# Three of sixteen drives per scan unit made by ScalarE on turned tiles, and the skip term and rectifier written to PSUM by ScalarE

## The reference

```
xp, z = split(x @ W_in)
xc    = silu(xprev * conv_w[0] + xp * conv_w[1] + conv_b)
dt_r, Bc, Cc = split(xc @ W_x)          # 8, 16, 16 columns
dt    = softplus(dt_r @ W_dt + b_dt)
for each state s:   h[t] = exp(dt[t] * A[s]) * h[t-1] + (dt[t] * xc[t]) * Bc[t, s]
                    y[t] += h[t] * Cc[t, s]
y     = (y + D * xc) * silu(z)
out   = y @ W_out
```

## Time and profile before

| what | value |
|---|---|
| median of 3 runs | 949.73 us |
| span of the profiled execution, first to last instruction | 947.3 us |
| PE busy | 834.3 us (88%) |
| DVE busy | 710.7 us (75%) |
| ACT busy | 508.3 us (54%) |
| POOL busy | 549.2 us (58%) |
| share of 16 DMA engines, the one data queue | 57.9% |

### The profile page before, as it was taken

How to read it: one execution, slowest core, us unless ns; L and a number is a source line. 1 busy time by engine, 2 the same in 40 slices (tenths; PEclk the granted TensorE clock), 3 DMA queues, 4 the chain that set the end, 5 groups by cost and what they waited for, 6 DMA issues and landing times. The chain is left out here.

```text
span 947.3 us, 10224 instructions
## 1 busy us (share of the span) xinstructions
PE 834.3 (88%) x3004; PEld 492.0 (52%) x3004; DVE 710.7 (75%) x767; ACT 508.3 (54%) x702; POOL 549.2 (58%) x373
## 2 busy tenths in 40 slices
PE   5579897979899898986687999989999999999996
PEld 1224342433334333332243555558888888888885
DVE  1999999999999999999965455546565665565664
ACT  4645666556566666643315446456555554555553
POOL 4678989999998998875736955312212211212210
PEclk9799999999999999997987999999999999999999
DMA  7969898889879898796609800002343342343341
GB/s 167 342 201 344 312 332 273 337 311 305 324 257 369 308 327 309 279 328 222 202 0 137 157 0 1 1 1 63 117 133 100 122 133 90 90 133 100 122 118 59
DMA packets 75349, 178.24 MB, mean 188 GB/s; under 512 B 24514, under 2 KB 25044, under 8 KB 75300
## 3 DMA queue, kind: packets, MB, share of 16 engines
q1 hardware_dynamic: 75316, 177.85, 57.9%
HBM read 175.57 MB, written 2.26 MB: 188 GB/s over the span
## 5 line engine op out<-in xcount | busy, mean ns | idle before, releaser
L455 POOL TENSOR_TENSOR prod<-hidden,c_wide 128x1024 f32<-128x1024 f32 x128 | 300.0, 2356 | 64.6 <-DVE hidden L888 60.5
L551 PE MATMUL ps_y<-prod,ident 128*128 128x512 f32 x512 | 244.2, 622 | 27.9 <-POOL prod L455 27.7
L888 DVE TENSOR_TENSOR_SCAN hidden<-decay,ps_d 128x1024 f32<-128x1024 f32 x92 | 209.9, 2281 | 8.3
L1920 PE MATMUL ps_conv<-hankel,u_high 128*128 128x512 f32 (+1 forms) x768 | 215.3, 361 | 0.0
L551 PEld LDWEIGHTS ps_y<-prod,ident 128*128 128x128 f32 x512 | 99.0, 198 | 169.2 <-issue 116.7
L1920 PEld LDWEIGHTS ps_conv<-hankel,u_high 128*128 128x128 f32 x768 | 138.6, 189 | 25.4 <-DVE u_t L1786 0.2
L1920 PE MATMUL ps_conv<-hankel,u_low 128*128 128x512 f32 (+1 forms) x384 | 138.1, 360 | 0.0
L2034 DVE TENSOR_TENSOR stack<-ps_conv,stack 64x512 fp32r<-64x512 f32 x128 | 88.2, 689 | 62.7 <-ACT stack L2001 60.2
L1751 POOL CAST block_mix<-even 128x256 fp32r (+1 forms) x32 | 12.7, 396 | 209.3 <-PE sums L1792 209.3
L2034 DVE TENSOR_TENSOR qk<-ps_conv,qk 64x512 fp32r<-64x512 f32 x128 | 88.2, 689 | 50.2 <-ACT qk L2001 47.5
L874 DVE TENSOR_TENSOR ps_d<-ps_x,b_wide 128x1024 f32<-128x1024 f32 x92 | 113.3, 1232 | 4.9 <-DMA b_wide<-bc_rows 0.4
(11 more groups left out here) (283 smaller groups left out, 1158.8 us busy)
## 6 DMA issues: line engine op xcount, KB each, us to landing
b_wide<-bc_rows SPq DMA_DIRECT2D x128, 512.0 KB, 5.6
c_wide<-bc_rows SPq DMA_DIRECT2D x128, 512.0 KB, 5.2
hankel<-filters SPq DMA_DIRECT2D x32, 1026.0 KB, 5.2
plus<-in_M_phi_plus SPq DMA_DIRECT2D x2, 1024.0 KB, 13.5
minus<-in_M_phi_minus SPq DMA_DIRECT2D x2, 1024.0 KB, 18.9
x_pair<-in_x SPq DMA_DIRECT2D x2, 768.0 KB, 8.5
bc_rows<-mixed_and_low SPq DMA_DIRECT2D x8, 128.0 KB, 5.4
out<-plus SPq DMA_DIRECT2D x4, 256.0 KB, 4.9
```

Of the source, the lines that this page charges most:

```text
L455: nc.gpsimd.tensor_tensor(prod[k % PAIR][:, :], hidden[k % DEEP][:, :], c_wide[s % BC_DEEP][:, :], ALU.mult).then_inc(prod_ready, 1)
L551: mm = nc.tensor.matmul(out, ident[:, :], halves(prod[k % PAIR])[h], start=False, stop=(k % N == N - 1))
L888: nc.vector.tensor_tensor_scan(hidden[k % DEEP][:, order], left[:, order], right[:, order], 0.0, ALU.mult, ALU.add).then_inc(hidden_ready, 1)
L1920: mm = nc.tensor.matmul(out, pairs[q][wp][:, 2 * delta + source, :], rows, start=(delta == 0 and term == 0), stop=(delta == 2 * half + 1 a ...
```

## The change

The drives of the states 4, 7 and 10 (`TURNED_STATES`) are no longer made by VectorE. `dtx` is turned once for each unit (tokens on partitions, 8 tiles of 128 by 128) together with B's rows; ScalarE copies both to SBUF (`dtx_t`, `b_t`). For each of the three states ScalarE then scales 8 tiles by one column of `b_t` each (a value for each token, `scale_drive`), and TensorE turns the 8 results back into `ps_d` (`turn_drive`), where the scan reads them. B's rows of these states are no longer spread by transfers, and the use of the `b_wide` buffers follows a table. The rectifier is written by ScalarE in place in `ps_w`, and `D * xc` is written by ScalarE into `ps_y`; TensorE adds onto both. `xc` is one buffer where there were two. In the last unit the shared states are 2 and 6 (before: 6) and the turned one is 7.

```diff
+TURNED_STATES = (4, 7, 10)
-        LAST_SHARE = POOL_STATES[2:3]
+        LAST_SHARE = (2, 6)
+        LAST_TURNED = (7,)
@@ TensorE
                 def gate_in(u, i, b):
-                    pe.wait_ge(dtx_ready, u)
+                    pe.wait_ge(dtx_t_ready, 3 * u)
                     project(i, b, w_gate[i], z_ready)
-                def add_rectified(u):
-                    pe.wait_ge(abs_ready, u + 1)
-                    pe.wait_ge(relu_ready, u)
-                    add_part(ident, rectified, start=True)
-                def skip_in(u, i):
-                    at_least(pe, gated_ready, u)
-                    for h, out in enumerate(halves(ps_y)):
-                        nc.tensor.matmul(out, skip[i][:, :], halves(xc[i])[h], start=True, stop=False)
+                def turn_dtx(u):
+                    def turn(half):
+                        for t in range(half * SPANS, (half + 1) * SPANS):
+                            mm = nc.tensor.transpose(ps_w[:, t * 128:(t + 1) * 128], dtx[:, t * 128:(t + 1) * 128], ident[:, :])
+                        mm.then_inc(dtx_turned, 1)
+                    pe.wait_ge(dtx_kept, u + 1)
+                    turn(1)
+                    for t in range(TILES):
+                        mm = nc.tensor.transpose(ps_w[:, t * C:(t + 1) * C], dt_low[BC_ROW:, t * 128:(t + 1) * 128],
+                                                 ident[BC_ROW:, BC_ROW:])
+                    mm.then_inc(dtx_turned, 1)
+                    pe.wait_ge(dtx_t_ready, 3 * u + 2)
+                    turn(0)
+                def turn_drive(u, s, last=False):
+                    scanned(u, s - 2)
+                    for half in range(2):
+                        pe.wait_ge(drive_t_ready, 2 * turned_before(u, s, last) + half + 1)
+                        for t in range(half * SPANS, (half + 1) * SPANS):
+                            mm = nc.tensor.transpose(ps_d[:, t * 128:(t + 1) * 128], drive_t[:, t, :], ident[:, :])
+                    mm.then_inc(drive_turned, 1)
...
                             if s == Y_LAG:
                                 if i == 0 and not first:
                                     out_product(b - 1)
+                                if Y_LAG + 1 in turned(not ahead):
+                                    turn_drive(u, Y_LAG + 1, not ahead)
+                                if i == 0 and not first:
                                     conv_in(v, j, bv)
-                                    pe.wait_ge(g.mixed_ready, b)
-                                skip_in(u, i)
...
-                                sum_states(n - Y_LAG, (k - Y_LAG) % (2 * N))
+                                sum_states(n - Y_LAG, (k - Y_LAG) % (2 * N), u if s == Y_LAG else None)
+                            if s > Y_LAG and s + 1 in turned(not ahead):
+                                turn_drive(u, s + 1, not ahead)
...
-                                if s == (7 if i == 1 or first else 5):
+                                if s == (7 if i == 1 or first else 6):
                                     scanned(u, WIDE_SHARED[1])
                                     low_rank(v, j)
...
-                                if s == 11:
-                                    add_rectified(v)
                                 if s == 12:
                                     add_exponential(v)
+                                if s == N - 1:
+                                    turn_dtx(v)
@@ ScalarE
+                def skip_in(u, i, taken=0):
+                    at_least(act, gated_ready, u)
+                    at_least(act, g.mixed_ready, taken)
+                    nc.scalar.activation(ps_y[:, :], xc[:, :], ACT.Copy, scale=cols[i][:, 1:2]).then_inc(skip_ready, 1)
...
-                        nc.scalar.activation(rectified[:, :], ps_w[:, :], ACT.Relu).then_inc(relu_ready, 1)
+                        nc.scalar.activation(ps_w[:, :], ps_w[:, :], ACT.Relu).then_inc(relu_ready, 1)
...
+                def take_turned(u):
+                    def take(n, half):
+                        act.wait_ge(dtx_turned, 3 * u + n + 1)
+                        nc.scalar.activation(dtx_t[:, half * SPANS:(half + 1) * SPANS, :].rearrange("p t d -> p (t d)"),
+                                             ps_w[:, half * H:(half + 1) * H], ACT.Copy).then_inc(dtx_t_ready, 1)
+                    at_least(act, drive_turned, TURNED * u)
+                    take(0, 1)
+                    act.wait_ge(dtx_turned, 3 * u + 2)
+                    nc.scalar.activation(b_t[:, :, :], ps_w[:, 0:H].rearrange("p (t c) -> p t c", c=C)[:, :, 0:N],
+                                         ACT.Copy).then_inc(dtx_t_ready, 1)
+                    take(2, 0)
+                def scale_drive(u, s, last=False):
+                    act.wait_ge(dtx_t_ready, 3 * u + 3)
+                    at_least(act, drive_turned, turned_before(u, s, last))
+                    for t in range(TILES):
+                        part = nc.scalar.activation(drive_t[:, t, :], dtx_t[:, t, :], ACT.Copy, scale=b_t[:, t, s:s + 1])
+                        if t % SPANS == SPANS - 1:
+                            part.then_inc(drive_t_ready, 1)
...
                                     else:
                                         norm_silu(nc, act, g, b - 1)
+                                skip_in(u, i, taken=b if i == 0 else 0)
                                 silu_input(v, j)
...
                                 decay_of(v, j, 1, last and i == 0)
+                                take_turned(v)
+                                if TURNED_STATES[0] in turned(last and i == 0):
+                                    scale_drive(v, TURNED_STATES[0], last and i == 0)
@@ VectorE
-                            if s in shared(final) and s in WIDE_SHARED:
-                                drive_step(u, s + 1, final)
-                            elif s not in shared(final) and not (s - 1 in shared(final) and s - 1 in WIDE_SHARED):
-                                drive_step(u, s, final)
+                            if s not in shared(final) + turned(final):
+                                drive_step(b, i, s, last)
```

More of the change, by code:

```diff
@@ L249, in mamba_stage @@
         soft = sb("soft", [D, L])
[L250 removed]
+        dtx_t = sb("dtx_t", [128, TILES, D])
+        drive_t = sb("drive_t", [128, TILES, D])
+        b_t = sb("b_t", [128, TILES, N])
         minus_ident = sb("minus_ident", [128, 128])
[L252 removed]
         one_plus = a.late[:, 0:L]
@@ L307, in shared_before, with turned_before, spread_order, b_slot @@
             return SHARE * u + sum(p < s for p in shared(last))
+        def turned_before(u, s, last=False):
+            return TURNED * u + sum(p < s for p in turned(last))
+        def spread_order(last):
+            return [(i, s) for i in range(2) for s in range(N) if s not in turned(last and i == 1)]
+        SLOT_ORDER = (0, 1, 2, 3) * 2 + (0, 1, 2) + (0, 1, 2, 3) * 3 + (0, 1, 2)
+        def b_slot(i, s, last):
+            at = spread_order(last).index((i, s))
+            return SLOT_ORDER[at] if at < len(SLOT_ORDER) else at - len(SLOT_ORDER)
+        def b_loads(b, i, s, last):
+            slot = b_slot(i, s, last)
+            rank = sum(b_slot(j, p, last) == slot for j, p in spread_order(last) if (j, p) < (i, s))
+            return 16 * (b * SLOT_ORDER.count(slot) + rank + 1)
         def own_states(last):
@@ L383, in unit @@
                     for s in range(N):
-                        spread_b(u, i, s)
+                        if s not in turned(u == 2 * B - 1):
+                            spread_b(u, i, s)
                         if u or s:
@@ L752, in batch @@
                                 decay_of(u, i, t, final)
+                            if t in turned(final) and t != TURNED_STATES[0]:
+                                scale_drive(u, t, final)
                             if t == N and not final:
@@ L962, in _ @@
                 nc.vector.tensor_scalar(minus_ident[:, :], ident[:, :], -1.0, None, ALU.mult).then_inc(minus_ready, 1)
-                for i in range(2):
-                    nc.vector.tensor_scalar(skip[i][:, :], ident[:, :], cols[i][:, 1:2], None, ALU.mult).then_inc(diag_ready, 1)
                 first_dt()
```

99 lines of the change are left out of this document (59 added, 40 removed).

## The result

The changed kernel takes 980.69 us (median; 978.97 to 982.32) where the kernel before takes 950.81 us (949.38 to 952.35) on the same chip: ratio 1.0311, 95% interval 1.0279 to 1.0343. The forecast was 977.5 us in a range of 956 to 1003.

What follows compares the result with a forecast made beforehand. VectorE was taken to bound the stage at 54.0 us a unit, GpSimd close behind. Forward units +0.6, backward +15.0, clock +14.1 and ends -1.7 made +28.0 on 949.7: 977.5 us, range 956 to 1003.

Steps and rivals of the forecast that it cites:

- Term 1: Boundary between units: sums and gate's projection stand behind the turning, scan 2 comes late; +1.8 us per unit with a successor.
- Term 2: Scan 7 in a forward unit waits for its turned drive: +2.3 us; such a unit +0.2 us in all.
- Term 3: Backward unit: input projection queued behind a sum awaiting the skip term; scans 6, 7, 10 late by 3.7, 2.1, 1.8 us.
- Term 4: TensorE's clock falls behind idle times: +1.7 us in three backward units, +1.5 us at six boundaries.
- The ends: Opening unit +0.7 us, last unit -2.4 us for two drives less and no gate's projection.
- (a): Turned drives come in time, so the kernel gets faster: some -25 us, 925 us; chance 0.10.
- (b): Transposes are no activity for TensorE's clock, which falls at each boundary: 998 us; chance 0.20.
- (c): TensorE's clock stays high everywhere while the late scans stand: 963 us; chance 0.17.
- (d): Weight loads don't hide behind transposes, 0.2 us more on each: +25 us more, over 1000; chance 0.04.
- (e): Late scans are made up since GpSimd and TensorE have caught up: near no change, 950 us; chance 0.06.

Runs made afterwards that it cites:

- Run 1: Changed kernel with TensorE turning `dtx` and B's rows behind the sum of state 13 instead of ahead of it: 963.01 us.
- run 2: Changed kernel with the input projection ahead of the first sum in backward units too, unit 1 left as it was: 969.29 us.
- run 6: Kernel before with only the skip product replaced by ScalarE's write of the skip term to `ps_y`, no turned drives: 961.90 us.
- run 10: Kernel before with the skip term written by ScalarE, and the input projection ahead of the first sum in all units but the opening one: 950.68 us.
- run 3: Changed kernel with two useless pairs of 512-column products on TensorE in the gap behind the gate's projection of backward units: 977.79 us.
- run 4: Changed kernel with 32 useless 128x128 transposes on TensorE in the gap behind the gate's projection of backward units: 979.63 us.
- run 9: Changed kernel, turned drives kept, with six orders of transposes, projection, decay and scalings changed to fill waits: 945.32 us, ratio 0.9947 to the kernel before.
- run 5: Changed kernel with the `dtx` transposes behind the sum of state 13 and the input projection ahead of the first sum in backward units: 956.68 us.
- run 7: Changed kernel with ScalarE's skip term ahead of the group norm's silu in backward units instead of behind it: 975.94 us.

## Why the prediction was right, and where it was off

**Direction and place.** All the waits named were found at the scans named. Unit 3, gains against waits: removed -3.9 (10.65 less the 14.5 us of waits leaves -3.9); boundary +1.8 and +1.5 for the clock = 3.3 (4.3: scan 2 starts 14.17 us behind the copy of `dtx`, 9.83 before); scan 6 +3.7 and +1.7 = 5.4 (6.4); scan 7 +2.1 (1.83); scan 10 +1.8 (1.80). Predicted 8.7, measured 10.65. (The last line of the sum has a slip: 949.7 + 28.0 is 977.7, not 977.5.)

**Term 1** is right where the clock is high: in units 1, 2, 4 and 6 scan 2 starts 11.43, 11.38, 11.55 and 11.43 us behind the copy of `dtx`, forecast 11.65. Run 1 shows the cause, since the same transposes behind one sum take 17.7 us off the time.

**Term 2.** Scan 7 of unit 4 waits 2.18 us, forecast 2.3. A forward unit also waits about 1 us for a `b_wide` transfer (1.03, 1.01 and 1.03 us in units 2, 4 and 6), which I had priced at nothing.

**Term 3.** The chain (norm's silu, skip term, first sum, input projection) is shown by run 2, which takes scan 6's wait to 0.91, by run 6, which makes it without turned drives, and by run 10, which cures it. Scan 6 waited 5.5 to 6.4 us, more than the 3 to 5 named: the low clock took in the input projection too (2.82 us in unit 3 and not 1.88), where I had priced one pair. Of the 30 us some 11 are the skip term's and some 19 the turned drives', an estimate by difference: run 6 costs 11 alone, and run 1, which eases only the drives, recovers 17.7. The rectifier in place and the single `xc` were not run alone; in unit 3 the silu that writes `xc` was released by the projection, not by a reader of `xc`.

**Term 4, the step that was mis-sized.** I spread 1.5 us over six boundaries, 9.0 us. Four of them lost nothing to the clock; unit 3 lost 14.17 - 11.55 = 2.6 us and unit 5 (13.98 us) 2.4, about 5 in all. The difference is TensorE's idle time ahead of the turning: 2.91 and 2.90 us in units 3 and 5, 1.75 in units 1 and 2, 1.54 and 1.53 in units 4 and 6. In backward units I had the clock fall in the gap behind the gate's projection; runs 3 and 4 show that filling that gap leaves the first sum at 3.75 us, since a second idle time, the wait for the skip term, follows. My own term 3 had that wait in it and term 4 didn't look at it.

**The ends.** The opening is 1.6 us shorter by the table, where +0.7 was forecast, but not by its work. The first `dt * xc` of the program starts at 22.29 us, before at 25.11, and this start moves between 22.3 and 25.1 in the profiles of all the kernels here; counted from it, the opening unit is 60.66 us against 59.41, +1.25. The last unit was forecast at -2.4 and came out at +0.2; that stays open.

**How near, and how much of it luck.** The units add up to +31.0 where +29.7 was forecast. The clock at the boundaries was put 4 us too high; the transfers in forward units (3 us at nothing) and the waits in backward units (10.1 us in unit 3 where 9.3 were forecast for scans 6, 7 and 10) were put too low. The places and the waits were foreseen; that the total came within some 3 us is in part luck, errors that cancel.

**The rivals.** (a) was right only in that its mechanism exists: with the orders of run 9 the drives are worth something, 4 us, not 25, for GpSimd and ScalarE's decays in `ps_w` stand close behind. (b) fell by run 4, and by the clock of 1.00 in unit 4. (c) fell by the clock of 0.87 in unit 3. (d) fell: 8 transposes took 1.04 to 1.09 us with their weight loads. (e) fell: the late scans were not made up, unit 3 is longer by its 14.5 us of waits less the 3.9 us of drives.

## What to carry to other kernels

A piece of work moved to an engine with free time costs what stands behind it in the two queues it now ties together: list, for each new wait, the instructions queued behind the waiter, and who needs them. Here 30 us of loss were orders of the lists, not work, and two moved calls took 24 of them back. When a wait goes, look for the next one at once (runs 2, 5 and 9 each lost part of their gain to it), and before an engine is relieved compare its busy time with the next engine's: 52.3 beside 51.6 us promised less than a single 1.2 us instruction.

## What the runs showed of the hardware

Transposes kept TensorE's clock at 1.00 (2.4 GHz) as products did, 3.66 us of the ones and 3.60 of the others ahead of the same gap in unit 3; behind the shorter gap of unit 1 only the products did. Ahead of the turning the granted clock was still 1.00 behind idle times of 1.53 to 1.75 us (units 1, 2, 4 and 6 of the changed kernel) and 0.50 (1.2 GHz) behind 2.91 and 2.90 us (units 3 and 5); in run 7 it fell with the first transposes behind 2.40 us in unit 3 and stayed at 1.00 behind 2.41 us in unit 5. It also fell in the gap of 4.53 us in unit 3, at 217.5, where 8.6 us of sums and a projection without a gap stood ahead of it (from 204.19).

Eight transposes of 128x128 take 1.04 to 1.09 us at the high level and 1.97 at the low one (unit 1, clock 0.50 throughout; the 1.79 of unit 3 begins at the high level), and ScalarE's 128x128 piece with a scale for each partition 387 ns, eight in 2.43 us, forecast 2.4:

```profile
99.00 1.97 PE L593 MATMUL ps_d<-ident,drive_t 128*128 128x128 f32 x8 [4.50 <-DVE hidden L985]
```

```profile
L809 ACT ACTIVATE drive_t<-dtx_t,b_t 128x128 f32<-128x128 f32 x144 | 43.9, 387 | 0.2
```
